# A reordered opening: head lengths without the rms, rates in one operation, activation tables loaded ahead, context pieces moved to the prologue

## The chip, the cores and the metric

The kernel runs on one core of one Trainium2 chip. Its time is the device time of the whole program in microseconds (us): 2831.26 us, the median of 3 runs (2829.81 to 2834.96). The engines are TensorE (PE, with its weight loads PEld), VectorE (DVE), ScalarE (ACT), GpSimd (POOL) and SyncE (SP), which here only issues transfers. Each engine works its own list of instructions in order and waits at semaphores for the others.

## What is computed

The reference is a decoder of two layers. The opening stage, the only one that the change touches, computes the first attention (a linear attention with weights that are updated at test time) and, beside it, keys and values of two later cross attentions from a context of 6404 rows. The part of the attention that matters here:

```python
q = rms_norm(q, q_norm_w)              # x * rsqrt(mean(x*x) + 1e-6) * w, over 128 columns
k = rms_norm(k, k_norm_w)
q = l2_normalize(to_heads(q))          # x / (norm(x) + 1e-5), over 32 columns of a head
k = l2_normalize(to_heads(k))
lr = softplus(hidden @ lr_proj_w.T + lr_proj_b + BASE_LR_INV)   # three rates per head and token
# then a scan over 4 chunks of 256 tokens: gradients of W0, W1, W2 with the rates l0, l1, l2,
# five Newton-Schulz rounds on each, W = renorm(W + dW, its first row norms)
```

The context part computes, for each of 52 tiles of 128 context rows, `k = y @ Wk + bk` and `v = y @ Wv + bv` for the first cross attention, and for the second one `kv = y @ Wkv` with every head of the keys divided by its length.

## The kernel before

`opening_stage` writes out five lists of instructions, one per engine. In each of them two things are interleaved by hand.

**The attention chain.** A prologue (layer norm of x, transposes, projection to qkv of 8 token tiles with a copy of each to SBUF, rms norm, head lengths, rates, transposes of q, k, v), then three updates (`for c in range(UPDATES)`: forward pass with a sigmoid, gradients, five rounds, renorm with a square root), then the tail (last outputs, layer norm, query projection, split of the queries into three bf16 parts `q_parts`, which go to memory as `q_dram` and are loaded again by `load_queries`). The stage ends with a barrier; the next one begins with loads of keys.

**The context pipeline.** The generator `context()` of each engine yields 4 times per tick, over 55 ticks (52 tiles and three ticks to drain), so 220 pieces. A call `fill(label)` takes the next pieces, as many as the table `FILLS...` gives for the label; all engines have the same table, so all stand at the same piece at the same label. In a tick PE does the matmuls of the first pair (L520, L521, piece 1), K (L528, piece 2), V (L532, piece 3) and the transposes of an earlier tile (L539, piece 4). ACT copies results out (L390, L399 to L403, L410, L416), DVE sums squares and scales keys (L732, L723, L716, and L704 masks a new chunk), POOL splits keys in parts (L317 to L320) and raises sums to the power -0.5 (L325). Many of these wait for each other: V waits for ACT's L403, the next L520 for ACT's L416, L399 for POOL's L320 of the tile before, L723 for POOL's L325.

The table has 37 pieces in the prologue, 50 in each of the three updates (12 in the gradient, 6 in each round, 8 in the renorm) and 26 in the tail; the 7 left are taken by `fill.rest()` at the very end.

SP issues all transfers from one list: inputs first, then for each pair of tiles the stores and the next context chunk, then the patches of three rows of memory (L284 to L286), the last store of keys and the 9 loads of `load_queries` (L110, L112).

In the prologue DVE waits for `from_pow` (POOL raises the mean squares to -0.5, `rms`), multiplies qkv by it (L772), then by the norm weights (L775), squares are taken on ACT (L441), summed per head (L791), rooted (L444), and q, k are multiplied by the reciprocal (L798). The 24 instructions of `rated` (L804) multiply one token tile each by one rate. ACT needs another activation table for the square root, exp, ln and sigmoid: a load (ACT_TABLE_LOAD) stands ahead of the first activation that needs it.

## Time and profile before

| | us |
|---|---|
| median of 3 runs | 2831.26 (2829.81 to 2834.96) |
| profiled execution: its own time | 2832.58 |
| profiled execution: span | 2830.8 |
| opening stage in it (to the next stage's first memset) | 367.4 |
| DVE busy in the whole span | 2091.2 (74%) |
| PE busy in the whole span | 2419.0 (85%) |

The profile is of one execution. Time is counted from the start of its span. A busy PE is not a PE at its peak, since matmuls overlap and their ends are modelled. Idle time of an engine counts only where the next thing in the chain is what it waits for. PEclk is the granted share of TensorE's full clock.

### The profile page before, as it was taken

Reading aid. Unit: us, or ns where it says so; the run is one execution under the profiler, and the core shown is the slowest. Engines: PE = TensorE matmul, PEld = TensorE weight load, DVE = VectorE, ACT = ScalarE, POOL = GpSimd, SP = SyncE. Lnnn points to the kernel's source line nnn. Section 1 sums busy time; section 2 is a strip of 40 time slices with the busy share of each in tenths; the row PEclk is TensorE's granted clock in tenths of the full one; section 3 lists DMA queues with packets and bytes.
Section 4 is the critical chain, followed back from the end, with each engine's and each line's share of the span. In section 5 each row is a group of like instructions: output and inputs, shape, how many; then the busy total and the mean of one; then the engine's idle time right before and its main releaser. Section 6 shows DMA issues by size and latency. Waiting matters only on the chain. (4 is left out here: it accounts for less than half of the span.)

```text
span 2830.8 us, 35253 instructions
## 1 busy us (share of the span) xinstructions
PE 2419.0 (85%) x10344; PEld 891.7 (31%) x10344; DVE 2091.2 (74%) x3087; ACT 1538.3 (54%) x1858; POOL 297.4 (11%) x330
## 2 busy tenths in 40 slices
PE   5888735999999978999566589999999999995997
PEld 3655400222222123444222223333333333332443
DVE  5666648999998024444597889999999999966665
ACT  5544546676767962333343566666666666652111
POOL 4655600000000000000054000000000000000000
PEclk8998955999999989999688589999999999997998
DMA  4333399000000106766000521112003010112000
GB/s 115 131 125 122 130 150 113 21 24 25 24 25 25 32 27 180 191 191 182 24 0 12 116 78 45 30 55 77 29 29 103 29 30 29 32 35 103 0 0 7
DMA packets 186252, 190.66 MB, mean 67 GB/s; under 512 B 18464, under 2 KB 158181, under 8 KB 184801
## 3 DMA queue, kind: packets, MB, share of 16 engines
q1 hardware_dynamic: 186125, 189.00, 25.9%
q8 instruction: 75, 1.23, 0.2%
q14 instruction: 52, 0.43, 0.1%
HBM read 144.05 MB, written 41.42 MB: 66 GB/s over the span
## 5 line engine op out<-in xcount | busy, mean ns | idle before, releaser
L2468 DVE TENSOR_TENSOR y_acc<-y_acc,y_probs 128x1024 f32<-128x1024 f32 x408 | 496.2, 1216 | 33.8 <-ACT y_probs L2164 23.5
L2164 ACT ACTIVATE y_probs<-y_E,y_mask_bias 128x1024 f32<-128x1024 f32 x416 | 440.8, 1111 | 66.1 <-PE y_E L2249 66.0
L1112 ACT ACTIVATE x_probs<-x_E 128x1024 f32<-128x1024 f32 x408 | 396.8, 1021 | 137.0 <-PE x_E L1158 134.6
L1253 DVE TENSOR_REDUCE x_maxima<-x_M 128x1 f32<-128x496 f32 x676 | 420.1, 667 | 25.7 <-PE x_M L1140 14.0
L2258 PE MATMUL y_O<-y_probs,y_values 128*64 128x512 f32 x1664 | 402.3, 604 | 0.0
L2248 PE MATMUL y_E<-y_qa,y_ks 128*128 128x512 f16 x832 | 319.2, 384 | 1.2 <-ACT y_copied L2140 1.2
L2249 PE MATMUL y_E<-y_qb,y_ks 66*128 66x512 f16 x832 | 317.5, 382 | 0.0
L2140 ACT ACTIVATE y_copied<-y_M 128x1024 bf16<-128x1024 f32 x164 | 167.8, 1023 | 210.0 <-PE y_M L2215 210.0
L2406 DVE TENSOR_REDUCE y_maxima<-y_M 128x2 f32<-128x1024 f32 (+1 forms) x195 | 238.5, 1223 | 35.6 <-PE y_M L2215 23.5
L1577 DVE TENSOR_TENSOR f_hidden<-f_act_out,f_spread 128x512 f32<-128x512 f32 x160 | 110.6, 692 | 169.5 <-ACT f_act_out L1461 162.0
L1158 PE MATMUL x_E<-qs,x_keys 128*128 128x512 bf16 x816 | 220.2, 384 | 4.8 <-ACT x_probs L1112 2.9
L1171 PE MATMUL x_O<-x_probs,x_values 128*32 128x512 f32 x1632 | 217.3, 605 | 0.6 <-ACT x_probs L1112 0.6
L1461 ACT ACTIVATE f_act_out<-f_b 128x512 f32<-128x512 f32 x160 | 95.4, 597 | 185.0 <-PE f_b L1493 185.0
L2215 PE MATMUL y_M<-y_ks,y_qa 64*128 64x512 f16 x742 | 148.6, 397 | 26.8 <-DVE y_maxima L2406 24.1
L1498 PE MATMUL f_b<-f_hidden,f_weights 128*128 128x512 f32 x320 | 164.1, 596 | 4.9 <-DVE f_hidden L1577 4.9
L1493 PE MATMUL f_b<-f_xnT,f_weights 128*128 128x512 f32 x320 | 165.1, 598 | 1.1 <-ACT f_act_out L1461 1.1
L1140 PE MATMUL x_M<-x_keys,qs 64*128 64x496 bf16 x338 | 136.5, 404 | 23.8 <-DVE x_maxima L1253 23.3
L2258 PEld LDWEIGHTS y_O<-y_probs,y_values 128*64 128x64 f32 x1664 | 101.5, 136 | 171.1 <-issue 164.0
L2674 PE MATMUL g_b<-g_w_in,g_xT 128*128 128x512 f32 x256 | 120.0, 611 | 23.5 <-ACT g_xT L2634 17.0
L1140 PE MATMUL x_M<-x_keys,qm 64*128 64x496 bf16 x338 | 136.6, 404 | 0.0
L2417 DVE TENSOR_TENSOR y_running<-y_running,y_copied 128x1024 bf16<-128x1024 bf16 x192 | 131.1, 683 | 3.7 <-ACT y_copied L2140 3.4
L2248 PEld LDWEIGHTS y_E<-y_qa,y_ks 128*128 128x128 f16 x832 | 81.5, 98 | 141.5 <-issue 45.5
(460 smaller groups left out, 3035.7 us busy)
## 6 DMA issues: line engine op xcount, KB each, us to landing
f_spread<-comb_dram SPq DMA_DIRECT2D x160, 256.0 KB, 3.9
y_values<-v_dram SPq DMA_DIRECT2D x208, 128.0 KB, 2.2
v_dram<-a_v_out SPq DMA_DIRECT2D x26, 512.0 KB, 2.7
k_dram<-a_k_parts SPq DMA_DIRECT2D x26, 512.0 KB, 3.3
x_values<-v_dram SPq DMA_DIRECT2D x100, 128.0 KB, 2.1
f_weights<-f_w_in SPq DMA_DIRECT2D x80, 128.0 KB, 2.3
y_ks<-k_dram SPq DMA_DIRECT2D x75, 128.0 KB, 2.7
v_dram<-a_v_out SPq DMA_DIRECT2D x26, 256.0 KB, 2.0
```

The source lines that it names most:

```text
L1112: nc.scalar.activation(probs[:, n % 2, 2 * g:2 * g + 2, :], psE[:, 2 * g:2 * g + 2, :], ACT.Exp).then_inc(exped, 1)
L1140: T.matmul(banks[j], q, ks[r, 4 * (u // 2) + 2 * h + j, CHUNK0 * c:CHUNK0 * c + CHUNK0], start=True, stop=True).then_inc(done, 1)
L1158: ins = T.matmul(psE[:, j, :], ks[:, 4 * (u // 2) + j, P * t:P * t + P], qs[:, u, j, :], start=True, stop=True)
L1171: ins = T.matmul(psO[32 * j:32 * j + 32, :], values[:, i, 32 * j:32 * j + 32], probs[:, n % 2, j, :], start=(t == 0), stop=(t == TILES0 - ...
L1253: V.tensor_reduce(maxima[:, 2 * h + j, qt, c:c + 1], psM[(2 * entry + j) % 3][:, 0:CHUNK0], AX.X, ALU.max).then_inc(max_done, 1)
L2140: A(out, scores, ACT.Copy).then_inc(S["spare_copied"], 1)
L2164: A(probs[:, i, :], psE[:, 2 * (i % 2):2 * (i % 2) + 2, :].rearrange("p a b -> p (a b)"), ACT.Exp, bias=mask_bias[:, bass.ds(c * TILES_IN_ ...
L2248: T.matmul(psE[:, 2 * slot + j, :], ks1[:, u // 2 % 2, keys], qa[:, u, j, :], start=True, stop=False)
L2249: ins = T.matmul(psE[:, 2 * slot + j, :], ks2[:, u // 2 % 2, keys], qb[:, u, j, :], start=False, stop=True)
L2258: ins = T.matmul(psO[u % 2][DH1 * j:DH1 * j + DH1, :], values[:, i, DH1 * j:DH1 * j + DH1], probs[:, i, 512 * j:512 * j + 512], start=Fals ...
L2406: V.tensor_reduce(maxima[:, u % 2, :, 2 * g, bass.ds(c, 1)], psO_pair[:] if (u, g) == (0, 1) else psM[:], AX.X, ALU.max)\
L2468: ins = V.tensor_tensor(acc[:, u % 2, :], acc[:, u % 2, :], probs[:, i, :], ALU.add)
```

## The change

What it does, in the order of the program:

1. Loads: the broadcast of the mask row `real` to 96 partitions is cut in two. The first 1664 columns are loaded where all 6656 were, the rest after the weights. `null_v` moves from the loads that the context waits for (`load_c`) to the others. DVE waits for the rest ahead of chunk 6.
2. Prologue on DVE: qkv is multiplied by the norm weights first, as soon as it is there; the squares of that are summed per head, so the length of a head is taken without the rms. The rms then multiplies the lengths (64 columns) ahead of the 1e-5, and their reciprocals behind it. The multiplication of 2048 columns by the rms goes.
3. `rated` is one instruction over 8 token tiles where there were 8.
4. ACT: the square root of the first weights' sums moves beside that of the head lengths. Dummy activations of one column (`table`) make the sigmoid table load directly behind each square root, and the square root's table in round 2 of each update.
5. Table of pieces: 54 in the prologue (37 before), 16 in the tail (26 and 7 left over before), the updates as before.

```diff
-FILLS = (("stats", 4), ("xn", 2), ("proj0", 4), ("proj1", 4), ("sums", 4), ("ms", 4), ("qk", 4), ("hs", 3),
-         ("tr0", 4), ("tr1", 4))
+FILLS = (("stats", 4), ("xn", 3), ("proj0", 4), ("proj1", 4), ("sums", 6), ("ms", 8), ("qk", 6), ("hs", 6),
+         ("tr0", 6), ("tr1", 7))
-FILLS_END = (("last0", 4), ("last1", 4), ("q_stats", 4), ("q_norm", 4), ("q_tr", 5), ("q_split", 5))
+FILLS_END = (("last0", 2), ("last1", 2), ("q_stats", 3), ("q_norm", 3), ("q_tr", 3), ("q_split", 3))
...
-        LOADS_C, LOADS = 9, 10
+        LOADS_C, LOADS = 8, 11
+        REST = slice(INVERT_AT[0].stop, KVP)
...
-                sp.dma_start(real[0:CTX, :], d.real_keys.partition_broadcast(CTX)).then_inc(spread_real, 16)
+                sp.dma_start(real[0:CTX, INVERT_AT[0]], d.real_keys[INVERT_AT[0]].partition_broadcast(CTX))\
+                    .then_inc(spread_real, 16)
...
+                sp.dma_start(real[0:CTX, REST], d.real_keys[REST].partition_broadcast(CTX)).then_inc(spread_rest, 16)
... (ACT)
-                e.wait_ge(to_sqrt, 1)
-                ACTIVATE(ninit[:], wn[:], ACT.Sqrt).then_inc(from_sqrt, 1)
                 e.wait_ge(s_evac, TILES)
                 ACTIVATE(sq[:], qkv[:, :, 0:256].rearrange("p t (a b) -> p t a b", a=2), ACT.Square).then_inc(s_sq, 1)
                 fill("sums")
                 e.wait_ge(s_abs, 1)
                 ACTIVATE(le[:], la[:], ACT.Exp).then_inc(s_exp, 1)
+                e.wait_ge(s_qk, 1)
+                e.wait_ge(to_pow, 2)
+                ACTIVATE(sq[:], qk[:], ACT.Square).then_inc(s_sq, 1)
                 fill("ms")
                 e.wait_ge(s_u, 1)
                 ACTIVATE(ll[:], lu[:], ACT.Ln).then_inc(s_ln, 1)
-                e.wait_ge(s_qk, 1)
-                ACTIVATE(sq[:], qk[:], ACT.Square).then_inc(s_sq, 1)
                 fill("qk")
                 e.wait_ge(to_sqrt, 2)
-                ACTIVATE(hn[:], hs[:], ACT.Sqrt).then_inc(from_sqrt, 1)
+                ACTIVATE(ninit[:], wn[:], ACT.Sqrt)
+                ACTIVATE(hn[:], hs[:], ACT.Sqrt).then_inc(from_sqrt, 2)
+                ACTIVATE(table[:], half[:, 0:1], ACT.Sigmoid)
...
+                        if r == 2:
+                            ACTIVATE(table[:], half[:, 0:1], ACT.Sqrt)
                         fill("A2")
...
                     ACTIVATE(wr[:], wn[:], ACT.Sqrt).then_inc(from_sqrt, 1)
+                    ACTIVATE(table[:], half[:, 0:1], ACT.Sigmoid)
... (DVE; fill("ms") now stands behind the reciprocal of lu)
+                V.tensor_tensor(qk[:].rearrange("p t a b -> p t (a b)"), qkv[:, :, 0:256],
+                                norm_w[:].unsqueeze(1).to_broadcast([P, TILES, 256]), ALU.mult).then_inc(s_qk, 1)
...
-                e.wait_ge(from_pow, 2)
-                step(V.tensor_tensor(qk[:], qkv[:, :, 0:256].rearrange("p t (a b) -> p t a b", a=2),
-                                     rms[:].rearrange("p (t a) -> p t a", a=2).unsqueeze(3)
-                                     .to_broadcast([P, TILES, 2, P]), ALU.mult))
...
+                e.wait_ge(s_sq, 2)
+                V.tensor_reduce(hs[:], sq[:].rearrange("p t a (h f) -> p (t a h) f", h=NH), AX.X, ALU.add)\
+                    .then_inc(to_sqrt, 1)
                 step(V.tensor_tensor(le[:], le[:], la[:], ALU.mult))
+                fill("qk")
...
+                step(V.tensor_tensor(heads(hn), heads(hn), by_rms, ALU.mult))
                 step(V.tensor_scalar(hn[:], hn[:], 1e-5, None, ALU.add))
                 step(V.reciprocal(hs[:], hn[:]))
+                step(V.tensor_tensor(heads(hs), heads(hs), by_rms, ALU.mult))
+                fill("hs")
...
-                    for t in range(TILES):
-                        ins = V.tensor_tensor(out[:, t, :].rearrange("p (h f) -> p h f", h=NH),
-                                              src[:, t, :].rearrange("p (h f) -> p h f", h=NH),
-                                              rate[:, t, :].unsqueeze(2).to_broadcast([P, NH, DH]), ALU.mult)
-                    return ins
+                    return V.tensor_tensor(out.rearrange("p t (h f) -> p t h f", h=NH),
+                                           src.rearrange("p t (h f) -> p t h f", h=NH),
+                                           rate.unsqueeze(3).to_broadcast([P, TILES, NH, DH]), ALU.mult)
```

The order on ACT behind the eight copies of qkv and their fill, first before the change (`a_sq` is the squares, `a_le` the exp of the rates, the others are context):

```order
L431 ACT_TABLE_LOAD
L431 ACTIVATE a_ninit<-a_wn 128x192
L433 ACTIVATE a_sq<-a_qkv 128x2048
L410 ACTIVATE a_ksq<-a_K 128x512
L416 ACTIVATE a_v_out<-a_V 128x512
L390 ACTIVATE a_k_parts<-a_T 128x4x128
L399 ACTIVATE a_kf<-a_V,a_bk 128x128
L400 ACTIVATE a_k_parts<-a_V,a_bk 128x128
L403 ACTIVATE a_v_out<-a_V 128x8x16
L436 ACT_TABLE_LOAD
L436 ACTIVATE a_le<-a_la 128x96
```

and the same place after it (the context lines are two further down in the file):

```order
L433 ACTIVATE a_sq<-a_qkv 128x2048
L418 ACTIVATE a_v_out<-a_V 128x512
L392 ACTIVATE a_k_parts<-a_T 128x4x128
L401 ACTIVATE a_kf<-a_V,a_bk 128x128
L402 ACTIVATE a_k_parts<-a_V,a_bk 128x128
L405 ACTIVATE a_v_out<-a_V 128x8x16
L412 ACTIVATE a_ksq<-a_K 128x512
L418 ACTIVATE a_v_out<-a_V 128x512
L392 ACTIVATE a_k_parts<-a_T 128x4x128
L436 ACTIVATE a_le<-a_la 128x96
L439 ACTIVATE a_sq<-a_qk 128x2048
```

Two table loads are gone, six pieces stand where four were, and the second squares follow the exp at once, ahead of the eight pieces of "ms".

The order on DVE in the tail, from the second layer norm to the first step of the query split (`a_kT` here holds a rest of the queries), before:

```order
L67 TENSOR_SCALAR a_xn<-x,a_moments,a_rstd 128x128 x8
L732 TENSOR_REDUCE a_ksum<-a_ksq 128x8
L716 TENSOR_TENSOR a_k_parts<-a_T,a_k_parts 128x4x128
L723 SCALAR_TENSOR_TENSOR a_kn<-a_kroot,a_K 128x512
L922 TENSOR_TENSOR x<-x,a_bo 128x1024
L732 TENSOR_REDUCE a_ksum<-a_ksq 128x8
L716 TENSOR_TENSOR a_k_parts<-a_T,a_k_parts 128x4x128
L723 SCALAR_TENSOR_TENSOR a_kn<-a_kroot,a_K 128x512
L732 TENSOR_REDUCE a_ksum<-a_ksq 128x8
L925 TENSOR_TENSOR a_kT<-a_qT,a_q_parts 128x1024
```

and after:

```order
L67 TENSOR_SCALAR a_xn<-x,a_moments,a_rstd 128x128 x8
L724 TENSOR_TENSOR a_k_parts<-a_T,a_k_parts 128x4x128
L928 TENSOR_TENSOR x<-x,a_bo 128x1024
L931 TENSOR_TENSOR a_kT<-a_qT,a_q_parts 128x1024
L932 CAST a_q_parts<-a_kT 128x1024
```

Seven of the eight context instructions between the layer norm and the split are gone from here.

The order on ACT at the end of an update (`a_wr` is the square root for the renorm, `a_sig` the sigmoid that begins the next update), before:

```order
L486 ACT_TABLE_LOAD
L486 ACTIVATE a_wr<-a_wn 128x192
L410 ACTIVATE a_ksq<-a_K 128x512
L416 ACTIVATE a_v_out<-a_V 128x512
L390 ACTIVATE a_k_parts<-a_T 128x4x128
```

and after:

```order
L491 ACTIVATE a_wr<-a_wn 128x192
L492 ACT_TABLE_LOAD
L492 ACTIVATE a_table<-a_half 128x1
L418 ACTIVATE a_v_out<-a_V 128x512
L392 ACTIVATE a_k_parts<-a_T 128x4x128
```

The load stands behind the root where it stood ahead of it, and the context piece with the squares comes ahead of the root.

## Rows read from the trace of the kernel before

**Rows 1.** Windows of prologue and tail: PE, PEld, DVE, ACT, POOL busy us (instructions), granted clock, DMA
```profile
0.00:78.45 78.45, 47.27 (x150) 26.44 (x151) 45.73 (x107) 42.10 (x78) 39.68 (x57) 0.83 0.42 115
...
314.12:367.37 53.25, 28.82 (x106) 16.80 (x104) 25.80 (x59) 20.61 (x45) 25.42 (x33) 0.76 0.42 141
```
**Rows 2.** Timeline of the start: start us, us, engine line op, [idle before, releaser]
```profile
12.14 2.07 PE L528 MATMUL a_K<-a_wkv,a_ctx_real 97*128 97x512 f32 x2 [12.14 <-DMA a_null_v<-null_v_in]
...
15.90 2.13 DVE L67 TENSOR_SCALAR a_xn<-x,a_moments,a_rstd 128x128 f32<-128x128 f32 x8
...
31.12 0.50 ACT L427 ACTIVATE a_qkv<-a_b 128x396 f32<-128x396 f32 x1 [0.17 <-PE a_b L555]
```
**Rows 3.** Issues of transfers in the first 20 us: size, us to landing
```profile
a_real<-real_keys_in SPq DMA_DIRECT2D x1, 624.0 KB, 6.5
```
**Rows 4.** Timeline of the prologue: L520 begins a tick
```profile
38.69 0.49 PE L520 MATMUL a_V<-a_ctx_in,a_wk 96*128 96x128 f32 x2 [2.84 <-ACT a_v_out L416]
...
43.23 0.49 PE L520 MATMUL a_V<-a_ctx_in,a_wk 96*128 96x128 f32 x2
...
45.33 2.29 DVE L772 TENSOR_TENSOR a_qk<-a_qkv,a_rms 128x2048 f32<-128x2048 f32 x1 [0.53 <-POOL a_rms L334]
45.37 2.53 POOL L317 TENSOR_TENSOR a_kr<-a_kf,a_k_parts 128x128 f32<-128x128 f32 x1
47.65 2.40 DVE L775 TENSOR_TENSOR a_qk<-a_qk,a_norm_w 128x2048 f32<-128x2048 f32 x1
...
51.48 0.37 ACT L399 ACTIVATE a_kf<-a_V,a_bk 128x128 f32<-128x128 f32 x1 [7.60 <-POOL a_k_parts L320]
...
56.69 0.80 PE L520 MATMUL a_V<-a_ctx_in,a_wk 96*128 96x128 f32 x2 [1.44 <-ACT a_v_out L416]
...
63.10 0.79 PE L520 MATMUL a_V<-a_ctx_in,a_wk 96*128 96x128 f32 x2 [0.43 <-ACT a_v_out L416]
```
**Rows 5.** The same view, the sums of squares and the end of the prologue
```profile
39.77 2.27 DVE L768 TENSOR_REDUCE a_ms<-a_sq 128x16 f32<-128x2048 f32 x1
...
64.34 2.29 DVE L798 TENSOR_TENSOR a_qk<-a_qk,a_hs 128x2048 f32<-128x2048 f32 x1
...
72.08 2.01 DVE L804 TENSOR_TENSOR a_xnT<-a_qk,a_lrate 128x128 f32<-128x128 f32 x8
72.35 0.58 POOL L320 TENSOR_TENSOR a_k_parts<-a_kf,a_zeros 128x128 bf16<-128x128 f32 x1
...
78.45 1.28 ACT L461 ACT_TABLE_LOAD   x1
79.75 0.60 ACT L461 ACTIVATE a_sig<-a_b 128x512 f32<-128x512 f32 x1
```
**Rows 6.** Timeline of the end of the third update
```profile
306.69 0.20 DVE L746 COPY a_wn<-a_gn 128x64 f32<-128x64 f32 x1
...
308.43 0.69 DVE L732 TENSOR_REDUCE a_ksum<-a_ksq 128x8 f32<-128x512 f32 x1 [0.94 <-ACT a_ksq L410]
...
309.03 0.25 DVE L895 TENSOR_SCALAR a_wr<-a_wr 128x192 f32<-128x192 f32 x1
```
**Rows 7.** Timeline of the tail
```profile
315.00 2.41 PE L672 MATMUL a_b<-a_qT,a_fast_bd 128*128 128x256 f32 x8
...
322.42 0.39 PE L520 MATMUL a_V<-a_ctx_in,a_wk 96*128 96x128 f32 x2
...
326.73 0.49 PE L520 MATMUL a_V<-a_ctx_in,a_wk 96*128 96x128 f32 x2 [0.25 <-ACT a_v_out L416]
...
350.26 1.22 DVE L925 TENSOR_TENSOR a_kT<-a_qT,a_q_parts 128x1024 f32<-128x1024 f32 x1
...
353.64 0.69 DVE L928 CAST a_q_parts<-a_qT 128x1024 bf16<-128x1024 f32 x1
...
355.56 0.66 SPq L276 DMA_DIRECT2D q_dram<-a_q_parts  x1
...
367.37 0.28 POOL L1069 MEMSET x_maxima<- 128x224 f32 x1 [10.93 <-POOLq L2820]
```

More of the change, by code:

```diff
@@ L187, in opening_stage @@
         wsq, wn, wr, wnew, ninit = [sb(n, [P, 3, DHID]) for n in ("wsq", "wn", "wr", "wnew", "ninit")]
-        half, mhalf = sb("half", [P, 3]), sb("mhalf", [P, 16])
+        half, mhalf, table = sb("half", [P, 3]), sb("mhalf", [P, 16]), sb("table", [P, 1])
         wq0, bq0, bq4, bo0 = sb("wq0", [P, P]), sb("bq0", [P, 1]), sb("bq4", [P, 1]), sb("bo0", [P, P])
@@ L200, in opening_stage @@
             sem(n) for n in ("squared", "v1_done", "v0_done", "k0_done", "hi_done")]
-        got_real, spread_real = sem("got_real"), sem("spread_real")
+        got_real, spread_real, spread_rest = sem("got_real"), sem("spread_real"), sem("spread_rest")
         inverted, masked = sem("inverted"), sem("masked")
@@ L699, in mask_chunk @@
                     def mask_chunk(n):
+                        if n == 6:
+                            e.wait_ge(spread_rest, 16)
                         if n in (0, 6, 13, 19):
@@ L788, in _ @@
                 step(V.tensor_tensor(lrate[:], lz[:], le[:], ALU.add))
-                fill("qk")
-                e.wait_ge(s_sq, 2)
-                V.tensor_reduce(hs[:], sq[:].rearrange("p t a (h f) -> p (t a h) f", h=NH), AX.X, ALU.add)\
-                    .then_inc(to_sqrt, 1)
-                fill("hs")
+                e.wait_ge(from_pow, 2)
                 e.wait_ge(from_sqrt, 2)
+                by_rms = rms[:].unsqueeze(2).to_broadcast([P, 2 * TILES, NH])
+                heads = lambda v: v[:].rearrange("p (t h) -> p t h", h=NH)
+                step(V.tensor_tensor(heads(hn), heads(hn), by_rms, ALU.mult))
                 step(V.tensor_scalar(hn[:], hn[:], 1e-5, None, ALU.add))
                 step(V.reciprocal(hs[:], hn[:]))
+                step(V.tensor_tensor(heads(hs), heads(hs), by_rms, ALU.mult))
+                fill("hs")
                 qk64 = qk[:].rearrange("p t a (h f) -> p (t a h) f", h=NH)
```

12 lines of the change are left out of this document (4 added, 8 removed).

## The prediction

> **What bounds the kernel now.** I read the windows first, then the timeline of the opening from its start to the next stage's first instruction. Everything behind the barrier at 367.4 us is unchanged and only moves by as much as the barrier does. So the question is when the barrier comes.
>
> Over the prologue no engine is full: of 78.45 us PE is busy 47.27, DVE 45.73, ACT 42.10, POOL 39.68 [rows 1]. The same holds for the tail (28.82 of 53.25 for PE). What takes the time is latency: a chain of attention steps, and between its steps the context pieces, which themselves wait from engine to engine. The tick is the unit. Where little disturbs it and PE's clock is high, L520 follows L520 after 4.54 us (38.69 to 43.23) [rows 4] and after 4.31 us (322.42 to 326.73) [rows 7]; I use 4.4. At the low clock a tick takes 6.4 us (56.69 to 63.10) [rows 4]: the L520 pair reads 0.80 there and 0.49 in the other rows. The longest tick, 13.5 us from 43.23 to 56.69, is the one with the two multiplications of qkv.
>
> **Part by part.** I cut the prologue in three and count pieces from the two tables.
>
> Start, to the last of the eight copies of qkv, which ends at 31.12 + 0.50 = 31.62 [rows 2]; 10 pieces before, 11 after. The first context matmul starts at 12.14, released by the transfer of `null_v` [rows 2]. Ahead of it lies the broadcast of 624 KB, which took 6.5 us to land [rows 3]. A quarter of it stays. The 468 KB that leave the head of the queue are 4.1 us at the 115 GB/s of the prologue [rows 1], and nothing if the landing is all latency; I take 1.4, and 0.5 for the release without `null_v` (one issue slot). That is 1.9 earlier for the first matmul, and for xn (15.90) with it. The eleventh piece (one more V ahead of the projection) takes about 2.0, so the copies end where they did: 31.7. Bounds: -1.5 to +1.
>
> Middle, from 31.6 to the multiplication by the head lengths (L798, 64.34) [rows 5]; 19 pieces before, 30 after, or 7.5 ticks. At 4.4 they are 33.0. Two places hold them up. DVE now does the weighting (2.40, as L775 [rows 4]) and three operations of 96 columns for the rates (an estimate of 0.5 each, between the 0.25 of L895 [rows 6] and the 0.69 of L732) ahead of the "sums" pieces; of 3.9 us ACT has work for 1.0, so 2.9. Then ACT stands at the new wait for the mean squares (`to_pow`, because the second squares overwrite the first) until DVE has done a context turn and the sum (2.27, L768 [rows 5]): 3.7 us, with all eight "ms" pieces queued behind it on ACT, and behind those PE's V and next L520. Sum 33.0 + 2.9 + 3.7 = 39.6, so 71.2 where it was 64.34. What goes is contained in this: the multiplication by the rms (2.29), the wait for it, and the tick in which POOL's split came to 2.53 for its first step and ACT waited 7.60 for POOL [rows 4]. The two new operations of 64 columns on DVE cost at most the 0.25 of L895 each; I put them inside the rounding of the 2.9.
>
> End of the prologue, from L798 to the first sigmoid (79.75 - 64.34 = 15.4 [rows 5]); 8 pieces before, 13 after: 1.25 ticks more, 5.5. `rated` as one instruction: L798 does 2048 columns in 2.29, so 1024 take about 1.15 where eight took 2.01 [rows 5], some 0.8 less, three times. I count it at nothing: PE's transposes and ACT's copies run beside it and end later; if that cover is gone it is up to -2.4. The sigmoid's load (78.45, 1.28) ends as the sigmoid can start anyway. So 71.2 + 20.9 = 92.1: the prologue is 12.4 longer.
>
> POOL beside DVE: its operation took 2.53 while L772 ran [rows 4], but 0.58 beside the eight short ones of `rated` [rows 5]. The Trainium skill (SBUF — State Buffer, "SBUF: two separate sides") has a rule that speaks against merging them: an operation of DVE with two SBUF inputs and one of GpSimd hold a shared port pair in turn, each for its whole instruction. By that rule each merged operation can stop POOL for 1.15 us; the sum would be up to 3.5 us higher. The other loads: between the first copies and the first update there are 5 table loads before and 3 after. The trace shows 1.28 for one (L461) [rows 5] with the activation right behind it. The Trainium skill (ScalarE: Activation LUTs, "What ACT_TABLE_LOAD costs") gives about 2.66 us for a switch, with a drain; by that figure two fewer would be an estimated 2.8 us more gain, which the row does not support.
>
> Updates: 50 pieces each as before, shifted by one piece of a tick. At the end of an update the sums are ready at 306.89 and DVE goes on at 309.03, 2.1 later, since its reduction waited 0.94 for ACT, which was behind the table load and the root [rows 6]. After the change those squares stand ahead of the root: about -1 per update. Against it, the square root's load now stands in round 2 (1.28 on ACT, half of it in ACT's idle time: +0.6), and the pieces between the last transpose and the next forward pass become K, V, transposes instead of L520, K, V: +0.5. I take 0 for all three, bounds -4 to +5 (three times 1.28 plus a little, on either side).
>
> Tail: from the last forward pass (315.00) to the query split (350.26) [rows 7]; 21 pieces, all with full work, before. After: 13, of which 8 belong to the drain and hold at most one instruction of an engine. 8 fewer pieces at 4.4 a tick are 8.8; 16 fewer full ones are 17.6. Between these I add up the chain's own steps with the durations that the timeline has for them: forward pass 2.4, sigmoid 0.6, two products 1.4, outputs 1.5, addition 0.4, two pieces on DVE 1.4, statistics 2.5, power 1.7, normalising 2.5, transposes 2.0, one piece on PE 1.1, copy 0.6, query matmuls 3.8 (at the low clock), copies 1.4: 23.3 instead of 350.26 - 315.00 = 35.3, so -12.0. Behind the split (353.64 + 0.69 = 354.33) it is 13.0 us to 367.37 [rows 7]. The store of the queries was issued at 355.56, 1.2 late, because SP waited for a key store; that one is done by now, and so is most of the next: -1.9. Tail -13.9, bounds -10.7 to -19.5.
>
> Sum: +12.4 + 0 - 13.9 = -1.5. The profiled execution took 2832.58 (its span is 2830.8), so 2831.1; the median of the runs shown is 1.3 below the profiled one, so 2829.8.
>
> **The rivals.**
>
> Full gain (2823). The pieces cost a plain tick and everything removed counts whole: 4.25 ticks more are 18.7, less 2.3 (rms multiplication), 1.9 (start), about 4 (POOL's two stalled steps of some 2.5 [rows 4]) and 2.4 (`rated`): +8.1 and not +12.4. With the tail's -13.9 and -1 for two of the renorms the sum is -7.8, so 2823. For it: no engine is busy above 61% in the prologue, and ACT waited 7.60 at one spot. Against it: the ticks are latency, and DVE's list is in a fixed order, with a new wait on ACT.
>
> Cold matmuls (2838), the one on the other side. The granted clock is 0.83 over the prologue [rows 1]. PE loses its work for some 5 us at ACT's new wait. If the clock drops there and does not come back, the 33 pieces behind it (8.25 ticks) run at 1.2 GHz, with ticks of 6.4 and not 4.4. That is 16.5 us at most; part of the 6.4 is attention work and not the clock, so I take half, 8.3: 2838. It decides when PE still idles between the pieces as it did around 60 us, where three ticks ran at the low clock. Against it: with 30 pieces PE has more to do in the same time.
>
> Blocked POOL (2833). The merged `rated` stops POOL's split three times, 1.15 each, +3.5 on a chain that waits for POOL. This stays within what counts as no change.
>
> **How the numbers follow.** A measurement of this kernel can tell a change of about 0.2%, 5.7 us: faster is below 2825.6, slower above 2836.9. The forecast as worked out has 0.32, blocked POOL 0.12, the full gain 0.36, cold matmuls 0.20. The first two are "same" for the most part. The forecast's own range, with a part of the terms' bounds going one way, is 2824 to 2836. For all cases: 2816 to 2840. Faster 0.38, same 0.42, slower 0.20.
>
> **What would show it.** The first sigmoid of the first update (79.75 now) at 92 for the forecast, 88 for the full gain, 99 and more for cold matmuls, with L532 at 1.9 us between 50 and 90. The last forward pass (315.00) moves with it, by 12 or so; if the difference between the two moves, the updates are not neutral. From it to the barrier 38 to 39 us where there were 52.4. First context matmul at 10.2, and an idle ACT of nearly 4 us ahead of the second squares. The forecast is wrong if the sigmoid comes before 89 or after 97, or if the tail shrinks by less than 11.

## The result and the profile after

| | before | after |
|---|---|---|
| median | 2832.11 us (2829.81 to 2834.96, 4 runs) | 2810.04 us (2809.51 to 2812.45, 4 runs) |
| ratio | | 0.9923, 95% interval 0.9906 to 0.994 |
| profiled execution | 2832.58, span 2830.8 | 2809.75, span 2808.0 |
| first sigmoid of the first update | 79.75 | 88.97 |
| sigmoid of the queries, behind the third update | 317.44 | 309.34 |
| three updates (sigmoid to sigmoid) | 79.11, 78.45, 80.13 | 74.81, 70.11, 75.45 |
| end of the opening (barrier) | 367.37 | 343.57 |

The change made the kernel 22 us faster. The forecast was 2829.8, with a range of its own of 2824 to 2836 and one of 2816 to 2840 with the rivals; 2810.0 lies below both. The barrier moved by 23.8: +9.2 in the prologue, -17.3 in the three updates, -15.7 in the tail. The forecast had +12.4, 0 and -13.9.

The windows of the three updates after (columns as in [rows 1]):

```profile
88.97:163.78 74.81, 65.86 (x313) 43.36 (x312) 52.51 (x103) 39.08 (x93) 47.95 (x67) 0.91 0.42 140
163.78:233.89 70.11, 61.41 (x313) 40.96 (x312) 52.06 (x103) 38.86 (x95) 44.45 (x62) 0.98 0.43 146
233.89:309.34 75.45, 64.43 (x318) 43.30 (x317) 52.05 (x103) 37.26 (x92) 46.95 (x66) 0.95 0.40 136
```

The same of before, which the forecast never asked for:

```profile
79.75:158.86 79.11, 66.82 (x311) 43.74 (x310) 52.93 (x103) 39.07 (x94) 47.97 (x67) 0.91 0.39 131
158.86:237.31 78.45, 66.09 (x315) 44.36 (x315) 53.18 (x103) 38.87 (x92) 43.44 (x61) 0.91 0.39 131
237.31:317.44 80.13, 68.89 (x316) 45.26 (x316) 51.69 (x101) 37.50 (x92) 45.91 (x65) 0.89 0.38 129
```

Every engine has the same work in an update, to within a few instructions, and DVE is busy for the same 52 to 53 us; PE is busy for less where its clock is higher. The update is shorter since something waits less or runs at a higher clock. A table by stretches (starts of VectorE's instructions in the timeline, us, three updates) shows where. In it A and M are the matrices that VectorE writes in each round (`a_A`, `a_M`), and "the turned weights" are the transposed new weights, which the next forward pass needs. From the first product of the gate to that of the queries the table sums to -19.0; the first product came 0.9 behind the sigmoid before and 2.6 after, which makes the -17.3:

| stretch | before | after | sum |
|---|---|---|---|
| first product of the gate to squares of the gradient | 15.2, 15.5, 16.4 | 10.8, 11.4, 10.8 | -14.0 |
| to the first normalised X, to the first A | 7.1, 7.3, 8.3 | 9.9, 7.1, 8.8 | +3.2 |
| five rounds, A to M | 36.7, 36.2, 36.6 | 36.3, 34.0, 36.8 | -2.4 |
| sum of the new weights to their last product | 8.7, 9.9, 8.4 | 6.7, 6.8, 6.4 | -7.1 |
| that product to the copy of the turned weights | 3.0, 3.0, 3.0 | 3.6, 3.2, 3.6 | +1.3 |

The first row in the timeline of VectorE before, second update. Its three pieces of the fill point "hid" stand between `dhb` and the first `t`:

```profile
161.19 0.68 DVE L834 TENSOR_TENSOR a_dhb<-a_sg,a_b 128x512 f32<-128x512 f32 x1
161.81 0.69 DVE L716 TENSOR_TENSOR a_k_parts<-a_T,a_k_parts 128x512 f16<-128x512 f32 x1
162.42 0.68 DVE L723 SCALAR_TENSOR_TENSOR a_kn<-a_kroot,a_K 128x512 f32<-128x512 f32 x1
164.99 0.69 DVE L732 TENSOR_REDUCE a_ksum<-a_ksq 128x8 f32<-128x512 f32 x1 [1.89 <-ACT a_ksq L410]
...
165.93 0.68 DVE L836 TENSOR_TENSOR a_t<-a_sg,a_sig 128x512 f32<-128x512 f32 x1
...
168.69 0.69 DVE L840 TENSOR_TENSOR a_dgb<-a_dgt,a_t 128x512 f32<-128x512 f32 x1
...
174.95 0.43 DVE L849 TENSOR_TENSOR a_gsq<-a_grad 128x192 f32<-128x192 f32 x1 [2.21 <-ACT a_grad L470]
```

TensorE at the same time. The K matmul whose squares VectorE wants stands behind both gradient products, and the third gradient product waits for `dgb` and then takes 2.08 where 1.03 is usual; the granted clock is 1.00 up to 169 and 0.50 from 170 to 172:

```profile
162.44 1.03 PE L614 MATMUL a_b<-a_dhb,a_xnT 128*128 128x256 f32 x4
163.30 1.02 PE L528 MATMUL a_K<-a_wkv,a_ctx_real 97*128 97x512 f32 x2
...
169.44 2.08 PE L614 MATMUL a_b<-a_dgb,a_xn 128*128 128x256 f32 x4 [3.81 <-DVE a_dgb L840]
```

After, second update. Here the three pieces are the normalised K, the sums with the next mask (its line left out) and an empty one, and none waits. From `dhb` to the first `t` it is 2.13 and not 4.74, and TensorE waits 1.25 for `dgb`. Over the three updates this step gives 8.2 of the 14.0; another 4.7 come behind `dgb`, where the third product took 1.62, 2.08 and 2.08 before and 1.13 each time after:

```profile
167.69 0.68 DVE L840 TENSOR_TENSOR a_dhb<-a_sg,a_b 128x512 f32<-128x512 f32 x1
168.29 0.68 DVE L731 SCALAR_TENSOR_TENSOR a_kn<-a_kroot,a_K 128x512 f32<-128x512 f32 x1
168.89 0.68 DVE L740 TENSOR_REDUCE a_ksum<-a_ksq 128x8 f32<-128x512 f32 x1
...
169.82 0.68 DVE L842 TENSOR_TENSOR a_t<-a_sg,a_sig 128x512 f32<-128x512 f32 x1
...
177.80 0.36 DVE L855 TENSOR_TENSOR a_gsq<-a_grad 128x192 f32<-128x192 f32 x1
```

```profile
173.33 1.13 PE L620 MATMUL a_b<-a_dgb,a_xn 128*128 128x256 f32 x4 [1.25 <-DVE a_dgb L846]
```

The theory (called P in what follows, for parity): a tick is four pieces, so the number of pieces ahead of an update decides which kind stands at each fill point. On VectorE they are, in order, nothing, the low part, the normalised K, the sums. An update has 50 pieces, so the place moves by two from one update to the next: odd stays odd. With 37 pieces ahead (odd) the last of the three "hid" pieces is the sums of the K that TensorE has in its own "hid" fill, or the low part of the K that it turns there; with 54 (even) what it needs was in the fill before. By this theory it is not how many pieces were moved that counts but that 17 is odd.

The lines that answer to those of before, prologue and tail. First matmul and xn [rows 2], the multiplication by head lengths and the rates [rows 5], the third update's end [rows 6], the tail [rows 7]:

```profile
10.01 2.05 PE L534 MATMUL a_K<-a_wkv,a_ctx_real 97*128 97x512 f32 x2 [10.01 <-DVE a_ctx_real L712]
...
13.74 1.36 DVE L67 TENSOR_SCALAR a_xn<-x,a_moments,a_rstd 128x128 f32<-128x128 f32 x5
...
29.96 0.50 ACT L429 ACTIVATE a_qkv<-a_b 128x396 f32<-128x396 f32 x1 [0.16 <-PE a_b L561]
...
44.48 1.91 ACT L439 ACTIVATE a_sq<-a_qk 128x2048 f32<-128x2048 f32 x1 [3.93 <-DVE a_ms L779]
...
70.62 2.28 DVE L806 TENSOR_TENSOR a_qk<-a_qk,a_hs 128x2048 f32<-128x2048 f32 x1
72.93 1.23 DVE L811 TENSOR_TENSOR a_xn<-a_qk,a_lrate 128x1024 f32<-128x1024 f32 x1
...
81.72 1.45 DVE L811 TENSOR_TENSOR a_sq<-a_qkv,a_lrate 128x1024 f32<-128x1024 f32 x1
...
88.97 0.60 ACT L464 ACTIVATE a_sig<-a_b 128x512 f32<-128x512 f32 x1 [0.28 <-PE a_b L613]
...
300.37 0.25 DVE L754 COPY a_wn<-a_gn 128x64 f32<-128x64 f32 x1
300.55 0.67 DVE L740 TENSOR_REDUCE a_ksum<-a_ksq 128x8 f32<-128x512 f32 x1
301.14 0.24 DVE L901 TENSOR_SCALAR a_wr<-a_wr 128x192 f32<-128x192 f32 x1
...
307.31 1.99 PE L678 MATMUL a_b<-a_qT,a_fast_bd 128*128 128x256 f32 x8 [0.83 <-DVE a_w1t_bd L913]
...
328.86 1.23 DVE L931 TENSOR_TENSOR a_kT<-a_qT,a_q_parts 128x1024 f32<-128x1024 f32 x1 [1.78 <-ACT a_q_parts L509]
...
343.57 0.29 POOL L1075 MEMSET x_maxima<- 128x224 f32 x1 [22.96 <-POOLq L2826]
```

### The profile page after: what moved, and what is told of

Same layout as the page of the kernel before. It is cut to its first block and busy times, and to the rows that moved or that the text cites. A ratio compares the mean times of both kernels' runs of the same rounds, so it can differ in the third digit from the quotient of the medians.

```text
span 2808.0 us, 35185 instructions
## 1 busy us (share of the span) xinstructions
PE 2398.5 (85%) x10287; PEld 881.1 (31%) x10344; DVE 2086.7 (74%) x3067; ACT 1536.6 (55%) x1863; POOL 294.7 (10%) x330
## 3 DMA queue, kind: packets, MB, share of 16 engines
q8 instruction: 75, 1.23, 0.2%
## 5 line engine op out<-in xcount | busy, mean ns | idle before, releaser
L1164 PE MATMUL x_E<-qs,x_keys 128*128 128x512 bf16 x759 | 211.3, 384 | 11.3 <-issue 4.9
L1146 PE MATMUL x_M<-x_keys,qs 64*128 64x496 bf16 x338 | 136.7, 404 | 23.8 <-DVE x_maxima L1259 23.3
```

Source lines behind the costliest of these rows:

```text
L1146: T.matmul(banks[j], q, ks[r, 4 * (u // 2) + 2 * h + j, CHUNK0 * c:CHUNK0 * c + CHUNK0], start=True, stop=True).then_inc(done, 1)
L1164: ins = T.matmul(psE[:, j, :], ks[:, 4 * (u // 2) + j, P * t:P * t + P], qs[:, u, j, :], start=True, stop=True)
```

## The experiments

Each was timed in five rounds against the kernel before on its own chip; "updates" is first sigmoid to the sigmoid of the queries in its trace. The kernel before had medians of 2832.2 to 2834.3 beside them. The profiled execution is one of those timed. In most kernels it is within 3 us of the median; with "hid" later it was 7.7 above it, with 48 pieces in an update 6.4 and with 53 ahead 6.4, so there the trace shows less gain, or more loss, than the median. "By the ratios" compares two changed kernels by way of the kernel before, each beside its own.

| kernel | pieces ahead | tables in the updates | updates | median | ratio (95%) |
|---|---|---|---|---|---|
| before | 37 | as needed | 237.7 | 2832.1 | |
| one piece more | 38 | as needed | 231.0 | 2822.9 | 0.9955 (0.9941 to 0.9969) |
| before, pieces moved | 54 | as needed | 224.7 | 2824.1 | 0.9968 (0.9956 to 0.9979) |
| after, no tables | 54 | as needed | 229.3 | 2818.1 | 0.994 (0.9926 to 0.9954) |
| before, tables | 37 | ahead | 247.7 | 2844.3 | 1.0033 (1.0021 to 1.0045) |
| after, pieces as before | 37 | ahead | 248.8 | 2839.6 | 1.0027 (1.0017 to 1.0037) |
| after, one piece less | 53 | ahead | 252.7 | 2836.4 | 1.0008 (0.9999 to 1.0017) |
| after, one piece more | 55 | ahead | 249.4 | 2840.9 | 1.0024 (1.0015 to 1.0034) |
| after | 54 | ahead | 220.4 | 2810.0 | 0.9923 (0.9906 to 0.994) |
| after, two pieces more | 56 | ahead | 217.1 | 2815.3 | 0.9939 (0.9926 to 0.9953) |

**One piece more in the kernel before.**

```diff
-... ("qk", 4), ("hs", 3),
+... ("qk", 4), ("hs", 4),
```

> The kernel before with one piece more in the last fill before the transposes of the prologue (hs 4 where 3 were), so 38 pieces where 37 were, and nothing else; the remainder of the tail takes 6 where 7 were. Theory P (parity): a tick is four pieces, an update 50, and the change shifts the pieces by 17, an odd number. With an odd number of pieces before the updates VectorE's third fill piece of hid is the sums of a tick whose K matmul TensorE has queued behind the two gradient products of the same fill point, so VectorE waits there before it forms the derivative of the gate. With an even number that wait goes: from the first product of the gate to the squares of the gradient 11 us in each update where 15.2, 15.5 and 16.4 were, -14 in all, and the total time falls by 10 to 15 us (2817 to 2822 beside 2832). Rival A (amount: the updates got shorter since more pieces were done before them, 4.25 ticks): one piece changes nothing, the three stretches stay at 15 to 16 us, total within 2 us of before. Rival T (table loads): nothing changes, since the loads stay where they were.

Measured: -10.9, with gradient stretches of 10.8, 11.4 and 10.8, as after. One piece out of 220, and nothing else, brought half of what the whole change did. The amount and the table loads are out as the cause of this part. In the trace the updates got 6.7 shorter: the gradient gave the same 14.0, and the other stretches took 7.3 back, 4.3 of it between the squares of the gradient and the first A.

**One piece less in the changed kernel** ("hs" 5 for 6).

> The changed kernel with one piece less in the prologue (hs 5 where 6 were): 53 pieces, an odd number, 17 - 1 = 16 more than before, the same piece of a tick at each fill point of the updates as before. Theory P (parity): the wait for the sums in front of VectorE's gate derivative comes back in each update, the stretch from the first product of the gate to the squares of the gradient goes from 10.8, 11.4, 10.8 to 15 to 16.5 us, and the total rises by 10 to 15 us over the changed kernel (2820 to 2825). Rival A (amount): 16 pieces of the 17 are still moved, total within 2 us of the changed kernel's 2810. Rival T (table loads): same as A.

Measured: 2836.4, 26 over the changed kernel (by the ratios 0.86%, 24 us), so the sign was right and the price (10 to 15) too low. The gradient stretches came back (15.2, 15.9, 15.8), but the renormalization (10.4, 10.4, 9.3, where 6.4 to 6.8) grew as well, and so did the third round (10.1, 9.6, 10.1, where 7.6 to 8.2).

**Tables asked for ahead, in the kernel before.**

```diff
+                        if r == 2:
+                            ACTIVATE(table[:], half[:, 0:1], ACT.Sqrt)
...
                     ACTIVATE(wr[:], wn[:], ACT.Sqrt).then_inc(from_sqrt, 1)
+                    ACTIVATE(table[:], half[:, 0:1], ACT.Sigmoid)
```

> The kernel before with the activation tables in the updates asked for ahead, and nothing else: a square root of one column in the third round, a sigmoid of one column right behind the root of the weight lengths. Theory P + T: the gradient stretches stay at 15 to 16 us; from the sum of the new weights to their last product 9.0, 9.9 and 8.4 (before: 8.72, 9.92, 8.38) lose one load of 1.28 us each or more, so the total falls by 4 to 7 us. Rival A: the loads were hidden, or what they free is taken by the pieces queued on ScalarE: within 2 us of before. Rival T alone (the loads explain all of the 17 us that the updates lost): total falls by 15 to 17 us.

Measured: +10.6; none of the theories had a rise. The timeline of ScalarE shows why. Before, the load of the root's table ended with the sums just ready: the root came 0.65 late.

```profile
146.84 1.28 ACT L486 ACT_TABLE_LOAD   x1
148.13 0.36 ACT L486 ACTIVATE a_wr<-a_wn 128x192 f32<-128x192 f32 x1
148.40 0.58 ACT L410 ACTIVATE a_ksq<-a_K 128x512 f32<-128x512 f32 x1
```

With the loads asked for ahead, the sigmoid's stands in front of the square that VectorE's fill "root" waits for, and the lengths of the weights wait behind that:

```profile
149.53 0.36 ACT L488 ACTIVATE a_wr<-a_wn 128x192 f32<-128x192 f32 x1 [0.69 <-DVE a_wn L749]
149.91 1.28 ACT L489 ACT_TABLE_LOAD   x1
151.21 0.20 ACT L489 ACTIVATE a_table<-a_half 128x1 f32<-128x1 f32 x1
151.32 0.58 ACT L410 ACTIVATE a_ksq<-a_K 128x512 f32<-128x512 f32 x1
```

```profile
151.93 0.69 DVE L735 TENSOR_REDUCE a_ksum<-a_ksq 128x8 f32<-128x512 f32 x1 [1.83 <-ACT a_ksq L410]
...
152.86 0.25 DVE L898 TENSOR_SCALAR a_wr<-a_wr 128x192 f32<-128x192 f32 x1
```

That is +0.9 per update; the root's load in the third round puts +1.0 or a little more there (9.06 to 10.05). Of the updates' +10 some 4 remain: 2.8 in the first two rounds of the second update and 1.0 between its first product and its first A. What makes these longer was not settled.

**The changed kernel without these two.**

```diff
-                        if r == 2:
-                            ACTIVATE(table[:], half[:, 0:1], ACT.Sqrt)
...
-                    ACTIVATE(table[:], half[:, 0:1], ACT.Sigmoid)
```

> The changed kernel without the two small activations in each update (the square root in the third round, the sigmoid behind the root); the one in the prologue stays. Theory P + T: from the sum of the new weights to their last product 6.7, 6.8 and 6.4 us become 8 to 9, and the next sigmoid comes 0 to 1.3 us later still: total +4 to +8 over the changed kernel's 2810. Rival A: within 2 us of it. Rival T alone: +15 to +17.

Measured: 2818.1, +8 (by the ratios +0.17%, 5 us), within the 4 to 8 of P with the tables, or just at its end. The renormalization took 7.3, 7.6 and 7.2, less than the 8 to 9 expected, so 2.2 of it is the loads themselves at this place; the updates in all took 8.9 more, and the rest of that lies in other stretches. The two small activations are a gain at 54 pieces and a loss at 37.

**The pieces moved, in the kernel before; the old table of pieces, in the changed one.** Only `FILLS` and `FILLS_END` are exchanged.

> The kernel before with the fill tables of the changed one (54 pieces in the prologue, 16 in the tail) and nothing else: head lengths still by way of the rms, eight operations per rate, no table asked for ahead. Theory P (parity): 54 is even, so the gradient stretches are 11 us each (-14 in all) as they were with 38 pieces, the tail is the changed kernel's (-16), and the prologue pays for 17 pieces with nothing against it, first sigmoid at 96 to 100 (+17 to +20 over before's 79.75); updates without the table edits as with 38 pieces, 228 to 229 us in all where 236 were. Total 2832 + 18 - 8 - 16 = 2826, 2821 to 2830. Rival C (the new order of the prologue's code is what made the updates short): updates stay at 236, total 2834. Rival A (amount): the updates fall by the whole 17, total 2817.

Measured: 2824.1, first sigmoid 98.34, updates 224.7, tail 34.7: all but the updates (3 to 4 less) as expected.

> The changed kernel with the fill tables of the kernel before (37 pieces, odd), so only the code of the prologue and the tables asked for ahead. Theory P: gradient stretches 15 to 16.5, the loads asked for ahead stand in front of a square that VectorE waits for (as in the kernel before with these loads alone, +10.6), updates 246 to 248 us, tail 52 from the last forward pass as before; the prologue alone gains: first sigmoid at 70 to 74. Total 2832 - 8 + 11 = 2835, 2830 to 2839. Rival C (the code made the updates short): updates about 219, total 2807.

Measured: 2839.6, first sigmoid 73.0, updates 248.8, all within 1 us of the ranges of theory P, but the total 5 above its sum of 2835. The edits to the code alone make the kernel slower by 0.27%. The code of the prologue is worth 6.8 at 37 pieces (79.75 to 73.0) and 9.4 at 54 (98.34 to 88.97); 17 pieces cost 16.0 in the new code (0.94 each). The tail is 49.9 and 50.0 with the old table and 34.2 to 34.7 with the new one, whatever the code.

**55 and 56 pieces.** "hs" 7 and 8.

> The changed kernel with 55 pieces in the prologue (odd), one more than it has. Theory P: slow like the one with 53: gradient stretches 15 to 16.5, updates 248 to 252 us, total 2832 to 2840. Rival A (more pieces ahead make the updates shorter, and 53 is on the wrong side of an edge): total 2808 to 2812. Rival Q (what counts is the place within the tick of four, not odd or even): 55 stands at 3 where the kernel before stood at 1 and the changed one at 2; the first and third update would be like the second of before, 78.4.

> The changed kernel with 56 pieces in the prologue (even, and a multiple of four: the first and the third update then stand where the second stands now, at 70.1 us, and the second where they stand now, at 73 to 75). Theory P: gradient stretches 11, updates 213 to 219, two pieces (2.2 to 3.2 us) more before the first sigmoid, two fewer in the tail (-2 to -3): total 2806 to 2812. Rival A or any theory in which 54 is a lucky number: 2820 or more.

Measured: 2840.9 and 2815.3, 1 and 3 above what I expected. 55 is slow like 53 (gradient stretches 15.9, 16.2, 15.6, updates 249.4), 56 fast like 54. Rival Q had 78.4 for the first and third update at 55; they took 81.9 and 85.6. At 56 the updates that begin at a multiple of four took 70.7 and 71.0, the other 75.4. At 56 the barrier came at 343.55, as in the changed kernel, and the stages behind it took 5.3 longer (2469.8 for 2464.4), 4.7 of it within the second cross-attention (from 1536.86 to 2548.04, where it was from 1537.54 to 2544.01, between two powers of its norms on POOL); which of its waits did that I did not trace.

**VectorE's wait taken away at 37 pieces.**

```diff
                     V.tensor_tensor(dhb[:], sg[:], B[2][:], ALU.mult).then_inc(s_grads, 1)
-                    fill("hid")
...
                     V.tensor_tensor(dgb[:], dgt[:], t3[:], ALU.mult).then_inc(s_grads, 1)
+                    fill("hid")
                     fill("dX")
```

> The kernel before with 37 pieces and one edit in the updates: on VectorE alone the fill point hid (three pieces) stands behind the gate's derivative instead of ahead of it; every other engine keeps its order. Theory P says that what an odd number costs is VectorE's wait inside this fill, in front of the derivative that TensorE's third gradient product needs. So from the first product of the gate to the squares of the gradient 11 to 13 us where 15.2 to 16.4 were, in each update; updates 237.7 become 225 to 230 in all, total time -8 to -12 (2820 to 2824). Rival Q (the place of the pieces matters elsewhere, in TensorE's or ScalarE's queue, not this wait): the stretch falls by less than 2 us, total within 3 us of before. Rival B (the sums, now behind the derivative, hold up the tick and TensorE's clock falls): slower than before.

Measured: 2816.8, ratio 0.9937 (0.9924 to 0.995), -17.5; more than expected (8 to 12). Stretches 11.0, 11.3, 10.8; updates 227.6, which is 10.1 less. The profiled execution, the slowest of the five (2824.5, the others 2815.5 to 2817.1), is 8 faster than the one of before, so the trace accounts for 8 of the 17.5 and not for the rest. The derivative now runs through, and TensorE's third product meets it without a wait:

```profile
157.28 0.68 DVE L834 TENSOR_TENSOR a_dhb<-a_sg,a_b 128x512 f32<-128x512 f32 x1
157.88 0.68 DVE L835 TENSOR_TENSOR a_t<-a_sg,a_sig 128x512 f32<-128x512 f32 x1
...
160.69 0.80 DVE L839 TENSOR_TENSOR a_dgb<-a_dgt,a_t 128x512 f32<-128x512 f32 x1
```

```profile
162.70 1.03 PE L614 MATMUL a_b<-a_dgb,a_xn 128*128 128x256 f32 x4
```

Every other engine kept its order and the number stayed at 37, so what makes the gradient long is this one wait; the odd number only puts it there.

**Every update at a multiple of four.** 56 pieces ahead; "wT" 1 (48 pieces in an update) or 5 (52, and 8 in the tail).

> The changed kernel with 56 pieces in the prologue and 48 in each update (wT 1 where 3 were), 20 in the tail. 56, 104 and 152 are multiples of four, so each update begins where the 70.1, 70.7 and 71.0 us ones of the measured kernels did, and has two pieces less: 68 to 70 us each, 204 to 210 in all where 220.4 were; first sigmoid at 91.8; tail with four more pieces, 34.2 + 4 to 5. To the barrier 331 to 341 where 343.6 were: total 2800 to 2810 (forecast 2804). Rival: the third phase effect is small (update lengths stay at 73 to 75 for two of three): 2812.

> The same with 52 pieces in each update (wT 5) and 8 in the tail: also multiples of four. Updates 70.8 + 1 to 3 each, 214 to 220 in all; tail 34.2 less 8 pieces at 1.1 to 1.25, 24 to 26, unless the tail's own chain ends later than its pieces, then 28 to 31. To the barrier 331 to 340: total 2797 to 2808 (forecast 2803). Rival: the five pieces ahead of the copy of the new weights hold up the next forward pass for their whole length, updates +4 to +5 each: 2812 to 2816.

Measured: 2809.6, ratio 0.9909 (0.9893 to 0.9924), and 2813.4, 0.9926 (0.9913 to 0.9939). With 48 the kernel is no slower than the changed one and not measurably faster; the total is at the upper end of what I expected, and with 52 it is 5 above, where the rival had it (2812 to 2816). With 48 the updates took 72.0, 72.5, 75.8 where I expected 68 to 70. All three have the short rounds (34.0 to 34.2 from A to M) and the short renormalization (6.8). But the gradient took 11.4, 12.9 and 13.2, with the granted clock at 0.50 behind `dgb` in the second and third (176 to 179, 248 to 250), and from the copy of the weights to the next product of the gate it was 5.8, 6.0 and 4.7 where 3.2 to 5.0 were. That the two pieces taken from "wT" left a hole there is my reading and not shown. With 52 the updates took 74.6, 72.9 and 75.9, and the copy of the weights came 5.1 to 6.2 behind their last product, where 3.2 to 4.0 were.

**Rates in eight operations each, in the changed kernel.**

```diff
-                    return V.tensor_tensor(out.rearrange(...), src.rearrange(...), ..., ALU.mult)
+                    for t in range(TILES):
+                        ins = V.tensor_tensor(out[:, t, :]..., src[:, t, :]..., rate[:, t, :]..., ALU.mult)
+                    return ins
```

> The changed kernel with each rate in eight operations, one for each tile of tokens, where one covers all eight (24 where 3 were). The forecast had put the merge at nothing. Three merged ones took 1.23, 1.49 and 1.45 us. Theory N (nothing): first sigmoid at 88.5 to 89.5, total within 2 us of the changed kernel's 2810. Rival M: the 21 more starts cost 0.05 to 0.15 us each on the chain, first sigmoid 90 to 92, total 2811 to 2813.

Measured: first sigmoid 91.59, 2.6 later (0.5 of it there before the rates); total 2814.0, ratio 0.9928 (0.9915 to 0.9942), not told apart from the changed kernel's. Merged they took 1.23, 1.49 and 1.45; apart:

```profile
73.62 1.85 DVE L812 TENSOR_TENSOR a_xn<-a_qk,a_lrate 128x128 f32<-128x128 f32 x8
...
82.10 2.47 DVE L812 TENSOR_TENSOR a_xnT<-a_qk,a_lrate 128x128 f32<-128x128 f32 x8
84.50 1.69 DVE L812 TENSOR_TENSOR a_sq<-a_qkv,a_lrate 128x128 f32<-128x128 f32 x8
```

**The tables' other sign.** VectorE's fill "root" moved behind the product that makes the new weights: at 37 pieces with tables; the same with "hid" moved too; and both moves in the changed kernel.

```diff
-                    fill("root")
                     e.wait_ge(from_sqrt, c + 3)
...
                     V.tensor_tensor(fast[:], wnew[:], ninit[:], ALU.mult).then_inc(s_wnew, 1)
+                    fill("root")
```

> The kernel before (37 pieces) with the tables of the updates asked for ahead, and VectorE's fill root (two pieces) behind the product that makes the new weights, where it stood ahead of the wait for their root. Theory W (the sign of the tables' effect hangs on this one wait): from the sum of the new weights to their last product 9.6, 10.7 and 9.3 us fall to 6 to 7.5; updates 247.7 become 234 to 242, total 2844 falls to 2828 to 2836. Rival G (the loads cost by the lower clock that they bring about elsewhere): the stretch falls but the total stays within 3 us of 2844.

> The kernel before (37 pieces), tables asked for ahead, with both of VectorE's fills moved: hid behind the gate's derivative, root behind the new weights. Theory W: the two waits and the loads are all that set the updates apart, so they take 215 to 225 us where the changed kernel's take 220.4, gradient stretches 11, renormalization stretches 6 to 7.5; total 2832 - 15 to - 20 = 2812 to 2817, 0 to 5 below the 2816.8 of the fill hid alone. Rival G: 2822 or more, worse than with hid alone, as the tables by themselves were (+10.6).

> The changed kernel (54 pieces) with the same two fills of VectorE moved. Theory W: at an even number neither fill waits for anything in these places, so the gradient stretches stay at 10.5 to 11.5; the two pieces of root (1.1 to 1.3 us) leave the chain of the new weights where the root is back already, so 6.7, 6.8 and 6.4 become 5.5 to 6.5: total 2806 to 2811. Rival: the pieces that now come later hold up TensorE, whose clock falls: 2812 to 2820.

Measured: 2835.4, ratio 1.0007 (0.9998 to 1.0016); 2824.7, 0.9969 (0.9956 to 0.9981); 2812.7, 0.9926 (0.9912 to 0.9939). The first has its total as theory W had it, 9 of the tables' 10.6 gone (by the ratios 7), with a renormalization of 6.7, 7.8 and 6.7. But its updates fell by 2.6 only, to 245.1, though the renormalization alone gave 8.4; of the 8.5 that its profiled execution lost, the rest lies ahead of the updates (1.1), in the tail (1.9) and behind the barrier (2.9), where nothing was moved. So the total does not bear theory W out. The same move without the tables was not run, so what of the 9 is the load's and what the fill's own two pieces stays open. The second is further off: the gradient stretches were short (11.0, 12.1, 11.8), but the updates took 229.8 where 215 to 225 were expected, and the total is 8 above that with "hid" alone. At 37 pieces the third round still costs 1.0 more in each update with the root's load in it, and the two moved pieces lengthen the next stretch by 0.5 to 1.4. So theory W explains the renormalization and not the whole sign. In the third the gradient took 9.7, 11.2 and 9.7 and the renormalization 6.3, 5.9 and 6.3, a little less than in the changed kernel, and the total did not fall: it lies in the rival's range (2812 to 2820) and not in W's (2806 to 2811), since the way from the squares of the gradient to the first A (+2.4), the rounds (+1.2) and the copy of the turned weights (+2.2) took back more than these two gave (updates 222.0). Whether the clock is the reason, as that rival has it, was not traced.

## Why the prediction was wrong

**Updates, "I take 0 for all three, bounds -4 to +5": the step that failed.** They gave 17.3. The shift by one piece of a tick was seen, and priced only at the renormalization and at the next forward pass. It was never followed through the gradient, where 14.0 of it lie: VectorE's queue at "hid" against TensorE's, which both tables and the code show without a run. The trace of before had it too: TensorE idle for 3.76, 3.81 and 3.76 behind `dgb`, 11.3 in all. The only waits read in an update were those of the renormalization [rows 6], since the updates have the same pieces before and after. One sign that the prediction named did catch it: the last forward pass should have moved by the sigmoid's 12; it came 7.7 earlier (307.31) while the sigmoid came 9.2 later. One piece more (-10.9), one less (+26) and the moved fill (-17.5) show the cause; that the tables alone cost 10.6 shows that they are not enough. By the table of experiments the two work together: tables ahead are worth 4 to 9 us of the updates at 54 pieces, and an even number 7 to 13 without them, 27 or more with them.

**The renormalization, "about -1 per update":** the stretch lost 7.1. Of these 2.2 are the loads (the changed kernel without them); the pieces moved alone gave 5.0 (7.3, 7.6, 7.2 in the kernel before with 54 pieces).

**Start:** first matmul 2.1 earlier (1.9 forecast). The copies ended at 30.46, 1.2 early and not level; the bound held.

**Middle:** the multiplication at 70.62 for 71.2; ScalarE idle 3.93 at the new wait for 3.7. The wait and its size were right. The sum came out right in part by luck: of the 2.9 ahead of "sums" ScalarE shows 1.37, and the two ticks there took 4.55 and 4.05, while the ticks behind the wait took 5.8, 4.9, 6.1 and 4.8 and not 4.4.

**End of the prologue:** 18.35 for 20.9. The merged rates counted at nothing gave 2.1 of it (4.2 us of VectorE for 6.0 when apart); the cover that was assumed for them, PE's transposes, did not hide it. The blocked POOL happened. Beside the second rate (80.31 to 81.80) one step of POOL took 1.29 and beside the third (81.72 to 83.17) the next took 1.32, where 0.43 and 0.46 are usual and 0.56 and 0.59 were taken with the rates apart. The power beside the head-length product and the first rate (70.62 to 74.16) took 3.57 where 1.65 is usual. What this cost the chain was not isolated; even so the merge gained the 2.1. The rows of POOL:

```profile
70.83 3.57 POOL L327 TENSOR_TENSOR a_kroot<-a_ksum,a_mhalf 128x8 f32<-128x8 f32 x1
...
78.03 1.65 POOL L327 TENSOR_TENSOR a_kroot<-a_ksum,a_mhalf 128x8 f32<-128x8 f32 x1
...
80.80 1.29 POOL L321 TENSOR_TENSOR a_kf<-a_kr,a_k_parts 128x128 f32<-128x128 f32 x1
82.17 1.32 POOL L322 TENSOR_TENSOR a_k_parts<-a_kf,a_zeros 128x128 bf16<-128x128 f32 x1
```

Each of the three ended 0.24 to 0.32 behind the VectorE operation beside it. By the rule of the Trainium skill (SBUF — State Buffer, "SBUF: two separate sides") the two engines hold the shared port pair in turn, each for its whole instruction. These rows agree with it; it would only have made the sum larger.

**Prologue in all:** +9.2, between the forecast's 12.4 and the full gain's 8.1. Its sigmoid at 88.97 is 1 from where the full gain put it (88), and 0.03 before the 89 ahead of which the forecast called itself wrong.

**Tail:** 35.26 became 21.55 up to the split (forecast 23.3), and 17.11 became 14.71 from there: -16.1 for -13.9, of right mechanism. The pieces alone did it (34.7 with the old code). Two counts ahead of the result were off by one; the first would only move the outer bound of the tail (17 full pieces fewer are 18.7 and not 17.6): of the 13 pieces 9 and not 8 belong to the drain (54 + 150 pieces are done ahead of the tail, and the first 208 are the 52 tiles). And the two orders on DVE show seven context instructions before and one after, so six are gone from between the layer norm and the split.

**Cold matmuls:** half of it happened. TensorE stood idle for 5.00 at the new wait, up to 47.12, and the granted clock was 0.50 from 43.4 to 56.6 (L526 at 49.88 and at 55.70 took 0.80). But it came back, which the rival had denied, and after a second such stretch from 67.4 to 70.8 (L538 at 69.14 took 1.70) again. Before, it was low for longer, from 46.3 to 70.2 and for 3 us at 40, so over the prologue the granted clock rose from 0.83 to 0.90.

Sum with measured terms: +9.2 - 17.3 - 15.7 = -23.8 at the barrier; the stages behind it took 1.0 more. The full gain had the prologue right to 1.1 and still missed the total by 13, since it had -2 for the updates.

Open is the part of the updates in which no wait differs by name: the same update code with 54 pieces and no tables took 224.7 in one kernel and 229.3 in the other, nearly all of it in the second update, whose windows differ in the granted clock. Their second updates, first the kernel before with the pieces moved, then the changed kernel without tables:

```profile
175.22:245.86 70.64, 61.36 (x313) 40.97 (x312) 52.25 (x103) 38.78 (x93) 44.33 (x62) 0.98 0.43 147
```

```profile
166.39:241.28 74.89, 67.43 (x313) 44.76 (x312) 52.65 (x103) 38.84 (x93) 44.99 (x64) 0.89 0.40 134
```

The granted clock is 0.98 in one and 0.89 in the other, with the same instructions; PE is busy 6 us longer and the update takes 4.2 more. What makes the clock fall in one and not the other was not settled, and four or five microseconds of any such comparison may be that.

## What to carry to other kernels

This is one kernel, so take it as a question to ask and not as a rule. Where one list of background work is dealt out at fixed points of several engines' programs, moving work ahead of a loop also turns what stands at each point inside it: count the shift modulo the length of the background's turn, follow each engine's queue at one or two points, and look for a piece that waits for work another engine has queued behind its own critical step. A fill point that stands between two critical operations belongs behind the one that another engine waits for; here moving one call was worth 0.6%. And ask how long each stage's waits are even where its instruction counts do not change.

## What the runs showed that I had not expected

A table load asked for ahead is not free where the engine's queue has other work: the same two small activations (1.28 for a load and 0.20 for the activation) gave 8 us (by the ratios 5) at 54 pieces and cost 10.6 at 37. And one piece out of 220 in the kernel before moved the time by 10.9 us, in the changed one by 26 and 31.
